# Where the value products of a graph attention layer are made: from the attention stage to the weighting stage

## The reference

```
h = layer_norm(x); q = h@Wq + bq; k = h@Wk + bk; v = h@Wv + bv
e = sum(q[d_all] * k[s_all]) / sqrt(16)          # 8 heads, edges and self loops
alpha = segment softmax of e over d_all
agg = segment_sum(alpha * v[s_all], d_all)       # zero where a node has no edge
x = x + agg@Wo + bo
x = layer_norm(x + ffn(layer_norm(x)))
```

## Time and profile before

| | us |
|---|---|
| median of 3 runs | 2598.07 (2591.76 to 2600.58) |
| the profiled execution | 2596.22 |
| its span, first to last instruction | 2594.5 |
| PE busy over the span | 2131.5 (82%) |
| DVE / ACT / POOL busy | 1990.0 / 1308.9 / 1238.0 |

### The profile page before, as it was taken

The page is one execution under the profiler, slowest core; times in us unless marked ns, Lnnn a source line. Parts: engine busy times, 40 slices in busy tenths (PEclk is TensorE's granted clock), DMA queues, the critical chain, the costliest instruction groups (busy, mean ns, idle before and its releaser), DMA issues. The chain is left out here.

```text
span 2594.5 us, 49618 instructions
## 1 busy us (share of the span) xinstructions
PE 2131.5 (82%) x14412; PEld 1724.0 (66%) x14412; DVE 1990.0 (77%) x7951; ACT 1308.9 (50%) x3068; POOL 1238.0 (48%) x1401
## 2 busy tenths in 40 slices
PE   3777777599978777599999138886499999999998
PEld 3555555499977777478777126664377777777776
DVE  4999999888867788688887766664577777777774
ACT  1899999733323445466665100000265666566565
POOL 2764444177737775465551007777433333333332
PEclk9999999899988999799999558997699999999999
DMA  3888888577749999444442035664323323333331
GB/s 92 265 254 243 241 242 245 173 211 200 201 139 298 292 298 295 131 135 121 125 126 63 12 81 148 189 190 152 122 86 111 109 100 109 110 104 105 110 102 50
DMA packets 372838, 413.95 MB, mean 160 GB/s; under 512 B 51578, under 2 KB 260366, under 8 KB 372570
## 3 DMA queue, kind: packets, MB, share of 16 engines
q1 hardware_dynamic: 335002, 340.50, 41.9%
q0 software_dynamic: 34496, 69.37, 10.6%
q10 hardware_dynamic: 3072, 0.92, 0.2%
HBM read 264.11 MB, written 179.90 MB: 171 GB/s over the span
## 5 line engine op out<-in xcount | busy, mean ns | idle before, releaser
L1724 PEld LDWEIGHTS p_y<-w,g_T 128*128 128x128 f32 x3136 | 365.4, 192 | 46.4 <-issue 24.2
L1724 PE MATMUL p_y<-w,g_T 128*128 128x128 f32 x3136 | 365.8, 275 | 0.0
L1717 PE MATMUL p_f<-nT,w 128*128 128x512 f32 x784 | 355.1, 596 | 0.0
L1742 ACT ACTIVATE nT<-p_n 128x512 f32<-128x512 f32 x98 | 58.5, 597 | 577.1 <-PE p_n L1732 577.1
L1707 POOL TENSOR_TENSOR rstd<-var,minus_half 128x4 f32<-128x4 f32 x98 | 113.6, 1159 | 450.3 <-ACT res L1755 450.2
L548 POOL DMA_INDIRECT x_dst<-in_x_dram,idx x196 | 193.7, 988 | 228.9 <-DMA edge_x<-x_dst 147.1
L1749 ACT ACTIVATE g_T<-p_f,bf 128x512 f32<-128x512 f32 x392 | 266.8, 681 | 32.2 <-PE p_f L1717 32.1
L1137 POOL DMA_INDIRECT x_src<-x_rows,idx x196 | 185.3, 945 | 163.7 <-DVE normed L1304 73.6
L1542 POOL DMA_INDIRECT x_rows<-xv,idx x196 | 210.7, 1075 | 86.1 <-issue 52.7
L902 POOL DMA_INDIRECT h_src<-h_table,idx x196 | 190.1, 970 | 105.6 <-issue 55.8
L1717 PEld LDWEIGHTS p_f<-nT,w 128*128 128x128 f32 x784 | 142.3, 192 | 142.1 <-issue 142.1
(11 more groups left out here) (303 smaller groups left out, 5746.2 us busy)
## 6 DMA issues: line engine op xcount, KB each, us to landing
xs<-x_rows SPq DMA_DIRECT2D x98, 512.0 KB, 3.6
x_in<-in_x_dram SPq DMA_DIRECT2D x98, 256.0 KB, 4.0
h_table<-h_rows SPq DMA_DIRECT2D x98, 256.0 KB
x_rows<-x_in SPq DMA_DIRECT2D x98, 256.0 KB, 2.7
out_dram<-res SPq DMA_DIRECT2D x98, 256.0 KB, 2.1
x_rows<-x_rows SPq DMA_DIRECT2D x50, 500.0 KB
edge_x<-x_dst SPq DMA_DIRECT2D x98, 128.0 KB, 3.1
h_own<-edge_x SPq DMA_DIRECT2D x49, 256.0 KB, 4.6
```

Of the source, the lines that this page charges most:

```text
L1717: e.matmul(p_f[ch][:], w_1[:, ch * P:(ch + 1) * P], nT[:, g % 2, :], start=True, stop=True).then_inc(f_prod, 1)
L1724: mm = e.matmul(p_y[g % 2][:, a * D:(a + 1) * D], g_T[:, g % 2, ch, a * P:(a + 1) * P], w_2[:, ch, :], start=(ch == 0), stop=(ch == FCH - 1))
```

## The change

The two value products leave `attention`. `srcT` is no longer a pair of buffers but holds all 49 groups in SBUF (the place that `values` had), and `dstT` has four slots and is stored to `edge_dT` in place of `edge_v`. `weighted` loads `edge_dT` into four slots and makes both value products itself, two steps ahead of `p_att`, into PSUM; VectorE multiplies the weights with them from PSUM. To find the PSUM banks, `p_att` and `p_out` have two each in place of three. The bias product there is now of three rows in bf16 (the fp32 bias split into three bf16 parts, which sum to it), and GpSimd makes the split before its loop, in 17 chained small instructions.

In `attention` ScalarE now scales the source tiles too, with scale and shift as for the destination tiles; the order of the loop bodies on ScalarE and VectorE is new.

```diff
@@ attention, sync
-                            e.wait_ge(vd_ready, k + 1)
-                            e.dma_start(group_of(edge_v, group(k)), v_dst[...]).then_inc(stored[k % ON], 16)
+                            e.wait_ge(dstT_ready, GT * (k + 1))
+                            e.dma_start(group_of(edge_dT, group(k)), dstT[:, k % ON, :]).then_inc(stored[k % ON], 16)
@@ attention, tensor: now p_q, p_ks, p_kd; then p_sum of the group before
-                            for j in range(GT):
-                                mm = e.matmul(p_vs[:, j * D:(j + 1) * D], srcT[...], w_vqk[:, 0:D], start=True, stop=True)
-                            mm.then_inc(vs_prod, 1)
-                            wait(e, vd_ready, k)
-                            for j in range(GT):
-                                mm = e.matmul(p_vd[:, j * D:(j + 1) * D], dstT[...], w_vqk[:, 0:D], start=True, stop=True)
-                            mm.then_inc(vd_prod, 1)
@@ attention, scalar: the order of one step after the change
+    AHEAD + 5: logits <- p_sum                      (was AHEAD + 4 and last)
+    AHEAD + 2: srcT[:, group(k), :] <- p_src
     AHEAD + 1: normed dst, 4 tiles                  (waits for shift_ready)
-    AHEAD + 3: values <- p_vs; v_dst <- p_vd
+    AHEAD + 3: qT <- p_q
+    AHEAD + 1: normed src, 4 tiles, Identity with scale=rstd, bias=shift
+    AHEAD:     std <- mv                            (was AHEAD + 1, before qT)
@@ attention, vector: the order of one step after the change
+    AHEAD + 1: rstd = 1 / std                       (waits for std_ready)
+    AHEAD:     statistics of the 4 dst tiles
     AHEAD + 1: rstd *= done_col
     AHEAD + 2: carry 3
     AHEAD + 1: shift
+    AHEAD:     statistics of the 4 src tiles
     AHEAD + 2: carry 2
+    AHEAD:     aggregates of the dst tiles
     AHEAD + 2: carry 1
-    AHEAD + 1: normed src, 4 tiles (tensor_scalar)
+    AHEAD:     aggregates of the src tiles
     AHEAD + 2: carry 0
     AHEAD + 3: the two products q*k
@@ weighted, sync
+                            wait(e, vd_prod, g - TN + 1)
+                            e.dma_start(dstT[:, g % TN, :], group_of(edge_dT, g)).then_inc(dst_in[g % TN], 16)
                             wait(e, scattered[g % VN], scattered.after(g % VN, GT * (g // VN)))
-                            e.dma_start(xv[:, g % VN, :, X2, :], group_of(edge_v, g)...)
                             e.dma_start(xv[:, g % VN, :, X1, :], edges_of(x_rows, g)).then_inc(xv_in[g % VN], 16)
@@ weighted, tensor, between p_att (AHEAD + 1) and p_out (AHEAD + 2)
+                        if at_step(n, AHEAD - 1):
+                            g = n - AHEAD + 1
+                            e.wait_ge(dst_in[g % TN], 16 * (g // TN + 1))
+                            wait(e, own_ready, g - 1)
+                            for j in range(GT):
+                                mm = e.matmul(p_vd[g % 2][:, at], dstT[:, g % TN, at], w_vqk[:, 0:D], start=True, stop=True)
+                            mm.then_inc(vd_prod, 1)
+                            wait(e, src_ready, g - 1)
+                            for j in range(GT):
+                                mm = e.matmul(p_vs[g % 2][:, at], srcT[:, g, at], w_vqk[:, 0:D], start=True, stop=True)
+                            mm.then_inc(vs_prod, 1)
@@
-                            e.matmul(p_out[g % 3][:], one_row[:], bias_row[:]..., start=True, stop=False)
+                            e.wait_ge(bias_ready, 1 + GT)
+                            e.matmul(p_out[g % 2][:], one_rows[:], bias_rows[:]..., start=True, stop=False)
@@ weighted, vector
-                                e.wait_ge(xv_in[g % VN], 32 * (g // VN + 1))
-                                e.tensor_tensor(split(w_own[...]), split(xv[:, g % VN, :, X2, :]), group_heads(g, 0), ALU.mult)
+                                e.wait_ge(vd_prod, g + 1)
+                                e.tensor_tensor(split(w_own[...]), split(p_vd[g % 2][:]...), group_heads(g, 0), ALU.mult)
-                                e.tensor_tensor(split(w_src[...]), split(values[...]), group_heads(g, HEADS), ALU.mult)
+                                e.wait_ge(vs_prod, g + 1)
+                                e.tensor_tensor(split(w_src[...]), split(p_vs[g % 2][:]...), group_heads(g, HEADS), ALU.mult)
```

More of the change, by code:

```diff
@@ L1070, in layer, with attention @@
             gathered.passed(AHEAD, GE if l else GE - EARLY, GT)
-        def attention(values, logits):
+        def attention(srcT, logits):
             SN, ON = 6, 4
@@ L1208, in _ @@
                     for n in range(STEPS):
+                        if at_step(n, AHEAD + 5):
+                            k = n - AHEAD - 5
+                            e.wait_ge(summed, k + 1)
+                            e.activation(logits[:, group(k) * GT:(group(k) + 1) * GT, :].rearrange("p j h -> p (j h)"),
+                                         p_sum[:, 0:GT * 2 * HEADS], ACT.Copy).then_inc(logit_ready, 1)
                         if at_step(n, AHEAD + 2):
@@ L1211, in _ @@
                             e.wait_ge(src_turned, k + 1)
[L1212 to L1225, removed]
+                            e.activation(srcT[:, group(k), :], p_src[:], ACT.Copy).then_inc(srcT_ready, 1)
                         if at_step(n, AHEAD + 1):
@@ L1287, in _ @@
                             e.reciprocal(rstd[:, k % 2, :], std[:, k % 2, :]).then_inc(rstd_ready, 1)
-                        if at_step(n, AHEAD + 2):
-                            carry(n - AHEAD - 2, 3)
+                        if at_step(n, AHEAD):
+                            e.wait_ge(dst_in[(n - AHEAD) % SN], 16 * ((n - AHEAD) // SN + 1))
+                            wait(e, mv_ready, n - AHEAD - 1)
+                            row_stats(n - AHEAD, 0)
                         if at_step(n, AHEAD + 1):
@@ L1480, in _, with weighted @@
                     e.tensor_tensor(self_weight, self_weight, top[:], ALU.mult).then_inc(alpha_ready, 1)
-        def weighted(values, alpha):
-            RN, VN = 6, 9
+        def weighted(srcT, alpha):
+            RN, VN, TN = 6, 9, 4
+            PARTS = 3
             with ExitStack() as c:
@@ L1534, in _, with chain @@
                 def _(e):
-                    e.memset(one_row[:], 1.0).then_inc(bias_ready, 1)
+                    steps = [0]
+                    def chain(ins):
+                        steps[0] += 1
+                        ins.then_inc(bias_step, 1)
+                        e.wait_ge(bias_step, steps[0])
+                    e.memset(one_rows[:], 1.0).then_inc(bias_ready, 1)
+                    chain(e.tensor_copy(left[:], att_bias[0:PARTS, :]))
+                    for n in range(PARTS):
+                        chain(e.tensor_copy(part[:], left[:]))
+                        chain(e.tensor_copy(back[:], part[:]))
+                        chain(e.tensor_scalar(own_part[:], back[:], ident[0:PARTS, n:n + 1], None, ALU.mult))
+                        if n == 0:
+                            chain(e.tensor_copy(split_bias[:], own_part[:]))
+                        else:
+                            chain(e.tensor_tensor(split_bias[:], split_bias[:], own_part[:], ALU.add))
+                        if n < PARTS - 1:
+                            chain(e.tensor_tensor(left[:], left[:], back[:], ALU.subtract))
                     for j in range(GT):
-                        e.tensor_copy(bias_row[:, j, :], att_bias[0:1, :]).then_inc(bias_ready, 1)
+                        e.tensor_copy(bias_rows[:, j, :], split_bias[:]).then_inc(bias_ready, 1)
                     for g in range(GE):
@@ L1836, in gnn_program @@
             logits = sb("logits", [P, T, 2 * HEADS], F32, att)
-            values = sb("values", [P, T, D], F32, att)
-            attention(values, logits)
+            srcT = sb("srcT", [P, GE, GROUP], F32, att)
+            attention(srcT, logits)
             softmax(logits, logits)
-            weighted(values, logits)
+            weighted(srcT, logits)
         ffn()
```

164 lines of the change are left out of this document (80 added, 84 removed).

## The result

| | before | after |
|---|---|---|
| median, us (4 runs of each) | 2595.95 | 2510.76 (2507.24 to 2511.5) |
| the profiled execution / its span | 2596.22 / 2594.5 | 2507.24 / 2505.5 |
| first gather of `attention` to its last logits | 365.2 | 290.6 |
| from there to the first scatter of `weighted` | 126.8 | 127.5 |
| first to last scatter | 269.1 | 255.2 |

The ratio is 0.9667, 95% interval 0.9646 to 0.9688. Of the 89 us of span that are gone, 74.6 lay in the attention stage and 13.9 between the first and the last scatter.

The account below looks back on a forecast made before the run. It took PE to bound attention and POOL weighting; after the change, a chain with clock falls sets attention's step, 6.08 us. 2596.22 - 40 (steps) - 2 (tail) = 2554 us profiled, median 2556, range 2534 to 2578.

Parts of the forecast that it names:

- The value products go ... 5.20 us a step are left: Attention, PE: without the value products, 1.78 of 6.98 us, PE has 5.20 us of work a step.
- A chain does: Attention: no engine's busy time sets the period; a loop through ScalarE and VectorE does, 5.71 us a step.
- from reciprocal to shift, 1.52 us: Attention, link of the loop on VectorE: 1.02 us now, one carry out, four tiles' statistics in, 1.52 us.
- the falls of the clock, 0.37 us a step: Attention, PE: clock falls to half in one of about three steps, each lengthening the chain 1.1 us: 0.37 us per step.
- the gap that I forecast: Attention, PE: idle behind the sums and ahead of the turns, 5.71 - 5.20 = 0.51 us per step.
- Tail of the attention stage, -2: Attention's end: PE owes less work after the last scaling, so 2 us less, bounds 0 and -4.
- I go by the row: Weighting, POOL: L1614, with one PSUM input, stretches scatters all the same, so 0 us gained; bounds -18 to +9.
- Rival 3: Weighting: operands from PSUM relieve the scatters, half of 18 us of stretch goes, 2547 us; chance 0.10.
- Weighting on PE, hidden: Weighting, PE: 4.87 us a group with the added value products, under POOL's 5.52, so cost 0.
- Start, 0: Weighting's start: chained GpSimd instructions hidden, first value products ahead of first `p_att`; between -2 and +3 us, taken as 0.
- Rival 1: Attention: the clock stays full, step 5.71 us, 60 us less with the tail, 2538 us; chance 0.20.
- Rival 2: Attention: the loop is longer, 6.46 us per step, 22 us less, 2576 us; chance 0.13.

Follow-up runs that it names:

- x4: Changed kernel with VectorE's shift ahead of the first carry in attention and `mate` made by four one-input instructions: 2496.51 us, ratio 0.9614.
- a1: Changed kernel with VectorE scaling the source tiles and the old ScalarE and VectorE orders kept; value products still moved: 2533.59 us, ratio 0.9745.
- c2: Changed kernel with two extra unused ScalarE instructions behind the source scaling in each attention step: 2534.9 us, ratio 0.9758.
- c1: Changed kernel with one extra unused ScalarE instruction between source scaling and root in each attention step: 2516.6 us, ratio 0.9694.
- c3: Changed kernel with three extra unused ScalarE instructions behind the source scaling in each attention step: 2538.06 us, ratio 0.9771.
- b2: Kernel before the change, with `mate` made by four one-input instructions in place of one with two SBUF inputs: 2593.94 us, ratio 0.9979.
- b1: Changed kernel with ScalarE copying both value products to SBUF in weighting, so `w_own` and `w_src` have two SBUF inputs: 2527.17 us, ratio 0.9733.
- x2: Changed kernel with `mate` made by four one-input instructions in place of one with two SBUF inputs: 2504.57 us, ratio 0.9644.
- x1: Changed kernel with ScalarE's root ahead of the source scaling in attention: 2518.08 us, ratio 0.9698.

## Why the prediction was wrong, point by point

- **"The value products go ... 5.20 us a step are left"**: right; x4 runs at 5.22. **"A chain does"** set the period: right, and it is the chain named, in the order named.
- **The first term that was mis-sized: from reciprocal to shift, 1.52 us.** It measured 1.22. I had taken the 1.02 of the earlier trace rows, with a carry out and the four statistics in. But the 1.02 held more than its instructions need. From the reciprocal to the next start it was 0.27 us (1254.72 to 1254.99 in before), and from the product with the mask to the next 0.21 (1255.26 to 1255.47), where, by my reading, a carry waited for the carry ahead of it. In after these two distances are 0.12 (1255.12 to 1255.24) and 0.09 (1255.99 to 1256.08): 0.27 of the 0.30. With the statistics' 0.75 and the carry's 0.26 that gives 1.22. What the first of them held before is open. It is not the order alone: a1, with the order of before, has 0.10 there (1253.30 to 1253.40); but there VectorE comes to the reciprocal from other work, while before it had been idle for 0.71 us. The other links were right to 0.02. The chain was 5.41, not 5.71; by the mean step that is (5.71 - 5.44) x 48 = 13 us.
- **The second, and the largest: the falls of the clock, 0.37 us a step, 18 us in all.** They measured nothing: the clock stayed at 1.00. They failed first by the chain. At 5.71 the gap would have been 0.51 us, and c2 with 0.55 has falls. At 5.41 it is 0.2, and c1 shows that even 0.36 leaves the clock at 1.00. But the price was wrong as well: in c2 a fall costs 0.74 us and not 1.1, and they are rarer, 0.17 us a step. So even with the gap that I forecast about half of these 18 us would not have come. The rule of the Trainium skill, *TensorE: Matmul & The Clock Gate*, section "HAM oscillation — how this bites in real kernels", that only much longer idle gaps cost the clock, gave the clock of the kernel after; but c2, c3 and a1, with no gap behind the sums over 1.0 us and a clock of 0.92 to 0.93, go against it. Both terms together, (6.08 - 5.44) x 48, are 31 (13 and 18) of the 47 us that the forecast lay above the profiled execution.
- **Tail of the attention stage, -2**: right; the stage as a whole lost 74.6 us, the step (6.92 - 5.44) x 48 = 71.0 of it, so -3.6, within its bounds.
- **"I go by the row" for the scatters, 0**: wrong, -13.9 us, within the bounds of -18 to +9. The scatter that ended together with L1614 at 1718.87 had started under `mate`. The coincidence repeats because L1614 starts 0.86 us behind `mate` (1717.33 to 1718.19) and both take 0.68: so L1614 ends 0.86 us behind `mate`'s end, and that is just when a scatter ends that `mate` has held up. The Trainium skill, *SBUF — State Buffer*, section "Who interferes with whom", says that a VectorE instruction with two SBUF inputs contends with GpSimd, and one with at most one input there does not, outside its 2-port modes, which it says `tensor_scalar` can enter. The table agrees: two SBUF inputs stretch, an operand from PSUM does not, and the one-input `tensor_scalar` pieces of b2 stretch too, though no run shows in which mode they ran. L1614, my witness against it, stretched none of the 22 scatters that started under it. Rival 3 was right in its mechanism, and 13.9 of the 17.6 us of stretch went where it had given half.
- **Weighting on PE, hidden**: right. VectorE and PE get through a group in 4.98 us (`w_own` at 1603.15 and 1608.13), against 4.87 worked out, under POOL's 4 x 1.31 = 5.24. **Start, 0**: 0.7 us more; within its bounds.
- Sum of the parts not forecast: 31 + 1.6 + 13.9 = 46.5 of the 47 us; the start takes 0.7 back, and about 1 us lies in the other stages. Rival 1 had the clock right but kept the chain of 5.71, and rival 3 had the scatters right; my list held them only one at a time. Rival 2's 2576 leaves out the tail's 2 us; with it, it is 2574.

## What to carry to other kernels

When an order changes, build the length of a chain from the start-to-start distance of each instruction in it where nothing waits, not from an old distance that may hold a wait. What slows a neighbour down is found by what is running when the slowed instruction *starts*, counted over the whole stage; coincidence at its end in one row proves nothing. In a loop over several in-order queues, put the instruction on which others wait ahead of the ones that themselves wait.

## What the runs showed of the hardware

- A GpSimd scatter that starts while a VectorE instruction with two SBUF inputs is running ends 0.86 us behind that instruction's end: up to 0.5 us later than its usual 0.985 us. With such operands restored (b1) the stretch was 19.3 us instead of 3.8 and the kernel took 2527.17 us instead of 2510.76. With one operand from PSUM none of 161 was stretched (`w_own`, `w_src` and the add, in after and x2).
- One SBUF input does not protect by itself: under the 128-column `tensor_scalar` pieces of b2, 27 of 27 scatters took 1.01 to 1.04 us. What helped is that a piece takes 0.28 us and not 0.68.
- Where a scatter and a VectorE instruction with two SBUF inputs start within 0.025 us of each other, the scatter keeps its 0.985 us and the instruction takes 0.70 to 0.75 us instead of 0.68.
- TensorE's clock: in c2, with 1.71 us of 8-column sums and a gap of 0.55 us in an undisturbed step of 5.77 us, it went to 0.50 about every fourth step; with gaps of 0.36 and 0.38 us (c1, x1) it stayed at 1.00. In the weighting stage it was 0.92 before and 1.00 after, with the value products where gaps had been; the bias product had changed there too, and no run parts the two.
- A fall cost little here, where the engine that it slows had gaps: 0.17 us a step in c2, 0.07 in c3. Most of what c2 and c3 lost against after, 0.50 and 0.59 us a step, is the longer chain itself.
